# Causal attention with whole-array sums, queries and keys copied to SBUF, squares on GpSimd, and the output norm's roots behind the query's

## The chip, the cores and the metric

The kernel runs on one core of one Trainium2 chip. The metric is the device time of one execution in microseconds (us), the median of several runs. The core has a matrix engine, TensorE (PE in the rows; PEld is its loading of weights), VectorE (DVE), ScalarE (ACT), GpSimd (POOL) and SyncE (SP), which issues most DMAs. Every engine runs its own list of instructions in order, and semaphores order the engines among each other. Operands lie in SBUF; TensorE's products land in PSUM, which has eight banks of 512 fp32 columns.

## What is computed

Two decoder layers over 64 sequences of 128 tokens with 128 channels. The change touches one of their six parts, the second layer's causal self-attention with 16 query heads of 64 and one shared head of keys and values:

```python
xn = layernorm(x, g1)
q = xn @ Wq.T
kv = xn @ Wkv.T
k, v = (kv[..., :DIM_HEAD], kv[..., DIM_HEAD:])
q = q.reshape(b, n, HEADS, DIM_HEAD).transpose(0, 2, 1, 3)
q = q * SCALE
q, k = (l2norm(q), l2norm(k))
...
sim = jnp.einsum('bhid,bjd->bhij', q, k)
...
sim = jnp.where(causal_mask, max_neg, sim)
attn = jax.nn.softmax(sim.astype(jnp.float32), axis=-1).astype(sim.dtype)
out = jnp.einsum('bhij,bjd->bhid', attn, v)
...
out = out @ Wout.T
return layernorm(out, g2)
```

The caller adds the result to x and norms the sum again. Everything is fp32.

## The kernel before

The program runs its parts one after another, each over all tokens: a state-space scan, a preparation of weights, cross-attention, a gelu network, causal attention (`causal_phase`), a single-head attention and a last network. Names of tiles begin with the part's letter, `d_` in causal attention. A tile is channels (128 partitions) by tokens.

`causal_phase` takes 32 groups of two sequences (256 tokens, `N`). Each engine's list is written by hand as a function `step` of eight slots (`k` from 0 to 7); `drive` calls it for the first groups, then in a loop whose body is two groups, then for the last ones. In the steps of group `g`, the engine does work of `g` itself (`main`), the norm, keys and first queries of `g + 1` (`front`), and the output of `g - 1` (`tail`). Small tables say which piece stands in which slot.

- **Pieces.** A group has five: piece 0 are the keys, 1 to 4 the queries of four heads each (two products of 256 columns into one bank `pq`). `project` makes a piece in slot `QUERY`. In slot `LENGTH`, ScalarE squares it (`squares`, from PSUM into `sq`), TensorE sums the squares over a head's 64 channels (`lengths`, into `pn`), and VectorE takes the maximum with a small number (into `ln`). In slot `UNIT`, ScalarE makes the inverse root with `Ln` and `Exp` (`roots`), and VectorE multiplies `pq` by it: line 1553 for keys (`kn`), line 1556 for queries (`qn`).
- **Units.** A group has four: eight heads of one sequence. In an even slot TensorE makes the scores (two products, even and odd heads on the upper and lower 64 rows of the array, line 1371); ScalarE takes `Exp` of each half (line 1513); GpSimd multiplies each half by the causal mask `keep` (line 1355). Three slots later, in an odd slot, `weighted` makes the sums with the values `vv` and with ones: four products of 64 output columns each, the even and odd heads side by side in one bank, `pattn` for values and `pden` for ones (line 1385). ScalarE makes 1/`pden` with `Ln` and `Exp`, VectorE multiplies (line 1583).
- **Output.** In slots 1 and 2, eight products add up the output of the group before into `pm`; slots 3 and 4 norm it (ScalarE's square, TensorE's mean at line 1453, `Ln`, `Exp`, VectorE's product at line 1589) and add x (line 1593); slot 5 takes the mean out (TensorE, line 1457), slot 6 makes the second variance (line 1461) and its inverse root (`Ln`, `Exp`), and slot 7 the product that is stored.

Every engine takes the pieces of a slot in the order in which `step` names them, so a wait in one piece holds what stands behind it on that engine.

## Time and profile before

| | before |
|---|---|
| runs (us) | 3443.01, 3429.18, 3422.32; median 3429.18 |
| profiled execution (us) | 3427.96, of it 3426.2 from first to last instruction |
| TensorE busy | 3085.8 us (90% of the span), 12374 products |
| ScalarE busy | 2024.2 us (59%) |
| VectorE busy | 1765.3 us (52%) |
| GpSimd busy | 1152.1 us (34%) |
| causal attention | from about 1740 to 2644 us of the span |
| in it, each engine in 2000 to 2100 us | TensorE 97.97, ScalarE 74.55, VectorE 38.77, GpSimd 36.78 us; clock 1.00 |

Busy time of TensorE counts each product from its start to its modelled end, and ends overlap the next start; how far apart starts are says more. An fp32 product stands in the trace as two passes, so "x4" is two products. In the order of time, rows of one line that follow each other are merged: start, time from the first start to the last end, engine, line, tiles, shapes, count. The time in brackets is the idle time of the engine before the row, and what ended it. A list of instructions shows the line, the operation and the tiles, with the semaphores waited for in brackets; `REGISTER_ALU` and `ISA` are steps of the engine's sequencer, which compute the value that a wait compares with.

### The profile page before, as it was taken

To read this page: it belongs to the slowest core of one execution; us is meant where nothing else is said; L and a number is where in the kernel's file an instruction comes from. 1 tells how busy PE (TensorE), PEld (TensorE's weight loads), DVE (VectorE), ACT (ScalarE), POOL (GpSimd) and SP (SyncE) were. 2 spreads that over 40 slices of the span, in tenths; PEclk is the share of its full clock that TensorE was granted. 3 is DMA by queue.
4 is the path that set the end of the run, shared out by engine and by line. 5 is a ranking of instruction groups with operands and counts; after the bars stand their busy time and mean duration, and the time that the engine had idled before them with its cause. 6 is when DMAs were issued, how large, how long until landed. Compare 5 with 4: busy or idle time off the path is not lost. (4 is left out here: it accounts for less than half of the span.)

```text
span 3426.2 us, 44444 instructions
## 1 busy us (share of the span) xinstructions
PE 3085.8 (90%) x12374; PEld 1646.6 (48%) x12374; DVE 1765.3 (52%) x2607; ACT 2024.2 (59%) x4072; POOL 1152.1 (34%) x954
## 2 busy tenths in 40 slices
PE   5888888799999999966779999999998879999998
PEld 2333333477777777722234444444444634444443
DVE  5999999455555555589933433333333521111111
ACT  5777776366666666545557777777775523333333
POOL 4788788122222222256623333333332100000000
PEclk8999999799999999988889999999999979999999
DMA  3545544000000000011100000000000300000000
GB/s 97 170 144 167 155 156 149 30 16 21 21 18 21 17 22 17 14 42 52 43 22 14 14 14 14 18 14 14 14 14 31 137 34 19 18 18 28 18 19 12
DMA packets 104265, 159.18 MB, mean 46 GB/s; under 512 B 11904, under 2 KB 44560, under 8 KB 104208
## 3 DMA queue, kind: packets, MB, share of 16 engines
q1 hardware_dynamic: 97872, 144.89, 12.5%
q10 hardware_dynamic: 6336, 13.60, 1.3%
q8 instruction: 26, 0.43, 0.1%
q14 instruction: 31, 0.25, 0.0%
HBM read 85.77 MB, written 4.72 MB: 26 GB/s over the span
## 5 line engine op out<-in xcount | busy, mean ns | idle before, releaser
L1355 POOL TENSOR_TENSOR d_pr<-d_pr,d_keep 128x512 f32<-128x512 f32 x256 | 320.4, 1273 | 566.7 <-ACT d_pr L1513 566.7
L770 POOL TENSOR_TENSOR b_pn<-b_e,b_inv 128x616 f32<-128x616 f32 x128 | 161.4, 1261 | 603.2 <-DVE b_inv L951 603.2
L256 POOL TENSOR_TENSOR a_bx<-a_bcopy,a_drive_u 128x512 f32<-128x512 f32 x256 | 320.2, 1271 | 18.1 <-DVE a_state L523 11.5
L523 DVE TENSOR_TENSOR_SCAN a_state<-a_decay,a_bx 128x512 f32<-128x512 f32 x256 | 311.0, 1215 | 5.7 <-POOL a_bx L256 5.4
L276 PE MATMUL a_py<-a_prod,consts 128*128 128x512 f32 x512 | 285.0, 640 | 2.8 <-DVE a_t L503 1.4
L1922 PE MATMUL f_ph<-f_hb,wb 128*128 128x512 f32 x512 | 232.8, 598 | 6.4 <-ACT f_hb L1955 6.4
L1922 PE MATMUL f_ph<-f_ha,wb 128*128 128x512 f32 x512 | 229.0, 596 | 2.3 <-DVE f_ha L1984 2.3
L454 ACT ACTIVATE a_decay<-a_delta,neg_a 128x508 f32<-128x508 f32 x256 | 174.5, 682 | 73.2 <-DVE a_state L523 73.0
L926 DVE TENSOR_REDUCE b_peak<-b_pscore 128x8 f32<-128x616 f32 x128 | 102.3, 799 | 215.7 <-PE b_pscore L807 215.7
L876 ACT ACTIVATE b_yy<-b_py,y_bias 128x154 f32<-128x154 f32 x512 | 169.4, 382 | 67.8 <-PE b_py L816 67.5
L1577 DVE TENSOR_SCALAR d_ln<-d_pn 128x512 f32<-128x512 f32 (+1 forms) x160 | 101.8, 636 | 197.6 <-PE d_pn L1408 197.6
L816 PE MATMUL b_py<-b_cf,wb 128*128 128x154 f32 x1024 | 191.1, 309 | 10.0 <-DMA b_cf<-ctx 5.4
L1408 PE MATMUL d_pn<-d_sq,consts 128*128 128x512 f32 (+1 forms) x320 | 168.8, 610 | 19.4 <-ACT d_sq L1476 18.9
L529 DVE TENSOR_TENSOR a_prod<-a_state,a_pc 128x512 f32<-128x512 f32 x256 | 175.9, 687 | 12.9 <-DVE a_state L523 1.0
L1513 ACT ACTIVATE d_pr<-d_pscore 128x512 f32<-128x512 f32 x256 | 139.0, 596 | 71.0 <-PE d_pscore L1371 69.4
L816 PEld LDWEIGHTS b_py<-b_cf,wb 128*128 128x128 f32 x1024 | 154.9, 191 | 52.7 <-issue 21.4
L1556 DVE TENSOR_TENSOR d_qn<-d_pq,d_ln 128x512 f32<-128x512 f32 x128 | 88.6, 692 | 173.0 <-ACT d_ln L1484 173.0
L288 PE MATMUL a_pc<-a_bc,sel 96*128 96x512 bf16 x256 | 106.4, 415 | 77.3 <-DVE a_prod L529 75.9
L889 ACT ACTIVATE b_pt_sb<-b_ptr 77x512 f32<-77x512 f32 x256 | 137.9, 588 | 50.2 <-PE b_ptr L825 50.2
L1981 DVE SCALAR_TENSOR_TENSOR f_th<-f_th,f_pa 128x512 f32<-128x512 f32 x64 | 44.0, 688 | 239.5 <-ACT f_th L1947 239.5
L1922 PEld LDWEIGHTS f_ph<-f_hb,wb 128*128 128x128 f32 x512 | 96.7, 191 | 135.0 <-issue 116.3
L1922 PEld LDWEIGHTS f_ph<-f_ha,wb 128*128 128x128 f32 x512 | 97.8, 191 | 126.8 <-issue 123.1
(281 smaller groups left out, 6492.0 us busy)
## 6 DMA issues: line engine op xcount, KB each, us to landing
a_bcopy<-rows SPq DMA_DIRECT2D x256, 256.0 KB, 3.5
wb<-in_wb ACTq DMA_DIRECT2D x14, 480.0 KB, 4.2
a_xf<-in_x SPq DMA_DIRECT2D x16, 256.0 KB, 4.2
a_xt<-in_x ACTq DMA_DIRECT2D x16, 256.0 KB, 3.6
x<-a_xo SPq DMA_DIRECT2D x16, 256.0 KB, 2.3
b_xf<-x SPq DMA_DIRECT2D x32, 128.0 KB, 2.0
b_xt<-x SPq DMA_DIRECT2D x32, 128.0 KB, 2.0
x<-b_xo SPq DMA_DIRECT2D x32, 128.0 KB, 2.0
```

Of the source, the lines that this page charges most:

```text
L256: gp.tensor_tensor(bx[:, k % 4, :], bcopy[:, k % 4, :], drive_u[:, p, :], ALU.mult).then_inc(*bxt.step("bx"))
L276: mm(py[:], S["ident"][:], prod[:, j % 4, :], start=j == 0, stop=j == SLOTS - 1).then_inc(*pey.step("y"))
L454: A(b4(decay[k % 2][:])[:, :, 1:SEQ], b4(delta[:, p, :])[:, :, 1:SEQ], ACT.Exp, scale=S["neg_a"][:, k:k + 1]).then_inc(*exp_t.step("decay"))
L523: V.tensor_tensor_scan(state[:, j % 2, :], decay[j % 2][:], bx[:, j % 4, :], 0.0, ALU.mult, ALU.add).then_inc(*vs.step("scan"))
L529: V.tensor_tensor(prod[:, j % 4, :], state[:, j % 2, :], pc[j % 2][:], ALU.mult).then_inc(*vs.step("prod"))
L770: gp.tensor_tensor(heads(pn[:, j % 2, :]), heads(e[:, j % 2, :]), over(inv[:, j % 2, :], CTX), ALU.mult).then_inc(*pnt.step("n"))
L816: op = mm(py[:, NC * h:NC * (h + 1)], W["at"][:, 128 * (2 * i + h):128 * (2 * i + h + 1)], cf[:, q, :], start=True, stop=True)
L876: op = A(yy[:, q, :, 2 * i + h, :], py[:, NC * h:NC * (h + 1)].rearrange("p (b k) -> p b k", b=NB), ACT.Identity, bias=S["y_bias"][:, 2 * ...
L1355: gp.tensor_tensor(half, half, keep[:].unsqueeze(1).to_broadcast([128, QP, SEQ]), ALU.mult).then_inc(*gmt.step(f"m{odd}"))
L1408: mm(pn[:, 0:w], S["pair"], sq[:, bank, 0:w], start=True, stop=True).then_inc(*pen.step("n"))
L1513: A(pr[:, j % 2, odd, :], pscore[:, 512 * odd:512 * (odd + 1)], ACT.Exp, scale=16.0).then_inc(*ext.step(f"e{odd}"))
L1922: op = mm(ph[k % 2][:], w[:, i, 128 * c:128 * (c + 1)], src, start=i == 0, stop=i == FC - 1)
```

## The change

Four things change in `causal_phase`.

1. **Sums.** `vv` holds ones, values, ones side by side for each sequence. `weighted` makes two products of 128 output columns: for even heads with values and ones, for odd heads with ones and values. `pattn` has two banks, one for even and one for odd heads; in each, half of the partitions are sums with values and the other half sums with ones. ScalarE takes `Ln` in two instructions of 64 partitions, and VectorE multiplies in two.
2. **Copies.** VectorE copies each piece of queries from `pq` to `qc` and the keys to `kc`, both in SBUF. `kn` and `qn` are made from the copies. `project` waits for the copy that frees its bank instead of for the product.
3. **Squares.** The queries' squares are made by GpSimd from `qc`, in the odd slots behind the masks; the keys' by ScalarE from `kc`.
4. **Order.** `project` stands ahead of `weighted` in the odd slots. The second variance's `Ln` and `Exp` move from slot 6 on ScalarE to slot 7 behind `roots`, and VectorE's last product ahead of the unit's sums.

```diff
+        qc = sb("qc", [128, 2, 2 * N])
+        kc = sb("kc", [128, N])
         qn = sb("qn", [128, 2, PAIRS, N])
-        vv = sb("vv", [128, 2, NB, DH])
-        ones = sb("ones", [128, DH])
+        vv = sb("vv", [128, 2, NB, 3, DH])
         keep = sb("keep", [128, SEQ])
...
-        pattn = ps("pattn")
-        pden = ps("pden")
+        pattn = ps("pattn", 1024)
...
+        def query(gu, i):
+
+            return UNITS * gu + i - 1
...
+                        if k % 2:
+                            if u := piece(QUERY, g, p, k, front, main):
+                                gu, pu, i, r, bank = u
+                                pool.wait_ge(*vcp.at("q", query(gu, i)))
+                                if begun(r - 2):
+                                    pool.wait_ge(*pen.at("n", r - 2))
+                                gp.tensor_tensor(sq[:, bank, :], qc[:, i % 2, :], qc[:, i % 2, :], ALU.mult
+                                                 ).then_inc(*psq.step("sq"))
...
-                    for bank, w in ((pattn, vv[:, p, b, :]), (pden, ones[:])):
-                        for odd in range(2):
-                            op = mm(bank[64 * odd:64 * odd + 64, :], w, pr[:, j % 2, odd, :], start=True, stop=True,
-                                    skip_group_check=True)
-                    op.then_inc(*pea.step("a"))
+                    for odd in range(2):
+                        w = vv[:, p, b, 1 - odd:3 - odd, :].rearrange("p i d -> p (i d)")
+                        mm(pattn[:, 512 * odd:512 * (odd + 1)], w, pr[:, j % 2, odd, :], start=True, stop=True
+                           ).then_inc(*pea.step(f"a{odd}"))
 
                 def project(gu, pu, i, r, bank):
...
-                    if begun(r - 2):
-                        pe.wait_ge(*vpt.at("unit", r - 2))
+                    if i == 2:
+                        pe.wait_ge(*kcp.at("k", gu))
+                    elif begun(query(gu, i) - (1 if i < 2 else 2)):
+                        pe.wait_ge(*vcp.at("q", query(gu, i) - (1 if i < 2 else 2)))
...
                 def lengths(gu, pu, i, r, bank):
-                    pe.wait_ge(*sqt.at("sq", r))
                     if i == 0:
+                        pe.wait_ge(*ksq.at("sq", gu))
                         pe.wait_ge(*vf.at("v", gu))
                     else:
+                        pe.wait_ge(*psq.at("sq", query(gu, i)))
                         pe.wait_ge(*vmx.at("max", r - 1))
                     w = N if i == 0 else 2 * N
...
+                        if k % 2:
+                            if u := piece(QUERY, g, p, k, front, main):
+                                project(*u)
...
-                        if u := piece(QUERY, g, p, k, front, main):
-                            project(*u)
+                        if k == 2:
+                            if u := piece(QUERY, g, p, k, front, main):
+                                project(*u)
...
-                    w = N if i == 0 else 2 * N
-                    act.wait_ge(*pep.at("p", r))
+                    act.wait_ge(*kcp.at("k", gu))
                     if begun(r - 2):
                         act.wait_ge(*pen.at("n", r - 2))
-                    A(sq[:, bank, 0:w], pq[bank][:, 0:w], ACT.Square).then_inc(*sqt.step("sq"))
+                    A(sq[:, bank, 0:N], kc[:], ACT.Square).then_inc(*ksq.step("sq"))
...
-                        if u := piece(LENGTH, g, p, k, front, main):
-                            squares(*u)
+                        if k == 3:
+                            if u := piece(LENGTH, g, p, k, front, main):
+                                squares(*u)
+                        if tail and k == 7:
+                            act.wait_ge(*peo.at("var2", g - 1))
+                            A(t3[:], pm[:, N:2 * N], ACT.Ln, bias=S["eps"]).then_inc(*so.step("ln2"))
+                            act.wait_ge(*so.at("ln2", g - 1))
+                            A(t3[:], t3[:], ACT.Exp, scale=-0.5).then_inc(*so.step("rstd2"))
                         if front and k == 0:
...
-                        if u := summed(g, p, k, main, tail):
-                            _, _, j, r = u
-                            act.wait_ge(*pea.at("a", r))
+                        done = summed(g, p, k, main, tail)
+                        if done:
+                            _, _, j, r = done
                             if begun(r - 1):
                                 act.wait_ge(*vat.at("n", r - 1))
-                            A(den[:], pden[:], ACT.Ln).then_inc(*sdt.step("ln"))
+                            for odd in range(2):
+                                act.wait_ge(*pea.at(f"a{odd}", r))
+                                op = A(den[64 * odd:64 * odd + 64, :],
+                                       pattn[64 - 64 * odd:128 - 64 * odd, 512 * odd:512 * (odd + 1)], ACT.Ln)
+                            op.then_inc(*sdt.step("ln"))
+                        if done:
                             act.wait_ge(*sdt.at("ln", r))
                             A(den[:], den[:], ACT.Exp, scale=-1.0).then_inc(*sdt.step("inv"))
                         if k == 4:
...
-                        if tail and k == 6:
-                            act.wait_ge(*peo.at("var2", g - 1))
-                            A(t3[:], pm[:, N:2 * N], ACT.Ln, bias=S["eps"]).then_inc(*so.step("ln2"))
-                            act.wait_ge(*so.at("ln2", g - 1))
-                            A(t3[:], t3[:], ACT.Exp, scale=-0.5).then_inc(*so.step("rstd2"))
...
                     for k in range(SLOTS):
+                        if k % 2 and k != 3:
+                            if u := piece(QUERY, g, p, k, front, main):
+                                gu, pu, i, r, bank = u
+                                dve.wait_ge(*pep.at("p", r))
+                                if begun(query(gu, i) - 2):
+                                    dve.wait_ge(*psq.at("sq", query(gu, i) - 2))
+                                    dve.wait_ge(*vpt.at("unit", r - 2 if i > 2 else r - 3))
+                                V.tensor_copy(qc[:, i % 2, :], pq[bank][:]).then_inc(*vcp.step("q"))
                         if u := piece(UNIT, g, p, k, front, main):
                             gu, pu, i, r, bank = u
                             dve.wait_ge(*spt.at("rstd", r))
                             if i == 0:
-                                V.tensor_tensor(kn[:, pu, :], pq[bank][:, 0:N], ln[:, bank, 0:N],
+                                dve.wait_ge(*kcp.at("k", gu))
+                                V.tensor_tensor(kn[:, pu, :], kc[:], ln[:, bank, 0:N],
                                                 ALU.mult).then_inc(*vpt.step("unit"))
                             else:
+                                dve.wait_ge(*vcp.at("q", query(gu, i)))
                                 V.tensor_tensor(qn[:, pu, 2 * (i - 1):2 * i, :].rearrange("p i t -> p (i t)"),
-                                                pq[bank][:], ln[:, bank, :], ALU.mult).then_inc(*vpt.step("unit"))
+                                                qc[:, i % 2, :], ln[:, bank, :], ALU.mult).then_inc(*vpt.step("unit"))
+                        if k == 3:
+                            if u := piece(QUERY, g, p, k, front, main):
+                                gu, pu, i, r, bank = u
+                                dve.wait_ge(*pep.at("p", r))
+                                if begun(query(gu, i) - 2):
+                                    dve.wait_ge(*psq.at("sq", query(gu, i) - 2))
+                                    dve.wait_ge(*vpt.at("unit", r - 2 if i > 2 else r - 3))
+                                V.tensor_copy(qc[:, i % 2, :], pq[bank][:]).then_inc(*vcp.step("q"))
+                        if tail and k == 7:
+                            dve.wait_ge(*so.at("rstd2", g - 1))
+                            if begun(g - 2):
+                                dve.wait_ge(store, 16 * g - 16)
+                            V.tensor_tensor(xo[:, q, :], pm[:, 0:N], t3[:], ALU.mult).then_inc(*vo.step("out"))
                         if front and k == 2:
...
+                        if front and k == 2:
+                            r = PIECES * (g + 1)
+                            dve.wait_ge(*pep.at("p", r))
+                            if begun(g):
+                                dve.wait_ge(*ksq.at("sq", g))
+                                dve.wait_ge(*vpt.at("unit", r - PIECES))
+                            V.tensor_copy(kc[:], pq[(1 - p) % 2][:, 0:N]).then_inc(*kcp.step("k"))
                         if u := summed(g, p, k, main, tail):
                             gu, pu, j, r = u
                             hh, b = j // 2, j % 2
                             dve.wait_ge(*sdt.at("inv", r))
-                            V.tensor_tensor(attn[:, pu, QP * hh:QP * (hh + 1), SEQ * b:SEQ * (b + 1)],
-                                            pattn[:].rearrange("p (i t) -> p i t", i=QP),
-                                            den[:].rearrange("p (i t) -> p i t", i=QP), ALU.mult
-                                            ).then_inc(*vat.step("n"))
+                            for odd in range(2):
+                                half = slice(64 * odd, 64 * odd + 64)
+                                op = V.tensor_tensor(
+                                    attn[half, pu, QP * hh:QP * (hh + 1), SEQ * b:SEQ * (b + 1)],
+                                    pattn[half, 512 * odd:512 * (odd + 1)].rearrange("p (i t) -> p i t", i=QP),
+                                    den[half, :].rearrange("p (i t) -> p i t", i=QP), ALU.mult)
+                            op.then_inc(*vat.step("n"))
                         if tail and k == 4:
```

Three places in the lists of the loop's body. First TensorE, slots 4 to 6, from the variance of the output (L1453, after the change L1474) to the scores of slot 6. Before:

```order
L1453 MATMUL d_pm<-d_t,consts 128x256 [waits d_so]
L1385 MATMUL d_pattn<-d_pr,d_vv 64x512 [waits d_vat,d_gmt]
L1385 MATMUL d_pattn<-d_pr,d_vv 64x512
L1385 MATMUL d_pden<-d_pr,d_ones 64x512 x2
L1397 MATMUL d_pq<-d_xn,wb 128x256 [waits d_vpt]
L1397 MATMUL d_pq<-d_xn,wb 128x256
L1456 ISA
L1457 MATMUL d_pm<-d_t,consts 128x256 [waits d_vo]
L1367 ISA
L1371 MATMUL d_pscore<-d_qn,d_kn 128x512 [waits d_vpt,d_ext]
L1371 MATMUL d_pscore<-d_qn,d_kn 128x512
```

and with the change:

```order
L1473 ISA
L1474 MATMUL d_pm<-d_t,consts 128x256 [waits d_so]
L1413 MATMUL d_pq<-d_xn,wb 128x256 [waits d_kcp]
L1413 MATMUL d_pq<-d_xn,wb 128x256
L1400 MATMUL d_pattn<-d_pr,d_vv 128x512 [waits d_vat,d_gmt]
L1400 MATMUL d_pattn<-d_pr,d_vv 128x512
L1477 ISA
L1478 MATMUL d_pm<-d_t,consts 128x256 [waits d_vo]
L1382 ISA
L1386 MATMUL d_pscore<-d_qn,d_kn 128x512 [waits d_vpt,d_ext]
L1386 MATMUL d_pscore<-d_qn,d_kn 128x512
```

The projection (L1397, now L1413) moved ahead of the sums (L1385, now L1400), and of the four sums two are left, with the whole array.

Second VectorE, from the keys' product in slot 4 to the queries' product in slot 5. Before:

```order
L1553 TENSOR_TENSOR d_kn<-d_pq,d_ln 128x256 [waits d_spt]
L1576 REGISTER_ALU
L1577 TENSOR_SCALAR d_ln<-d_pn 128x512 [waits d_pen]
L1588 ISA
L1589 SCALAR_TENSOR_TENSOR d_t<-d_pm,wb,d_t 128x256 [waits d_so]
L1591 ISA
L1592 REGISTER_ALU [waits d_vo]
L1593 TENSOR_TENSOR d_t<-d_t,d_xt 128x256 [waits d_load_t]
L1551 ISA
L1556 TENSOR_TENSOR d_qn<-d_pq,d_ln 128x512 [waits d_spt]
```

and with the change:

```order
L1587 REGISTER_ALU [waits d_spt]
L1588 TENSOR_TENSOR d_kn<-d_kc,d_ln 128x256 [waits d_kcp]
L1626 TENSOR_SCALAR d_ln<-d_pn 128x512 [waits d_pen]
L1647 ISA
L1648 SCALAR_TENSOR_TENSOR d_t<-d_pm,wb,d_t 128x256 [waits d_so]
L1650 ISA
L1651 REGISTER_ALU [waits d_vo]
L1652 TENSOR_TENSOR d_t<-d_t,d_xt 128x256 [waits d_load_t]
L1578 REGISTER_ALU
L1582 COPY d_qc<-d_pq 128x512 [waits d_vpt,d_psq,d_pep]
```

`d_kn` reads the copy `d_kc` instead of `d_pq`, and in front of it stands a step of its own that waits for the roots (`d_spt`); behind the addition (L1593, now L1652) comes the copy of the next queries (L1582), and only then `d_qn`.

Third GpSimd, where before only pairs of masks (`d_pr`) followed each other, slots 0 to 1 of the loop's body with the change:

```order
L1362 TENSOR_TENSOR d_pr<-d_pr,d_keep 128x512 [waits d_ext]
L1360 REGISTER_ALU
L1362 TENSOR_TENSOR d_pr<-d_pr,d_keep 128x512 [waits d_ext]
L1367 REGISTER_ALU
L1369 ISA [waits d_vcp]
L1370 TENSOR_TENSOR d_sq<-d_qc 128x512 [waits d_pen]
```

Behind each pair of masks stands one square (`d_sq`), which waits for VectorE's copy (`d_vcp`) and for the lengths that last read its buffer (`d_pen`).

## Rows read from the trace of the kernel before

**Rows 1.** Windows of a middle stretch: busy time (instructions) by engine, granted clock, DMA.
```profile
core 0: us, PE busy (x) PEld busy (x) DVE busy (x) ACT busy (x) POOL busy (x), PEclk, DMA share, GB/s
...
2000.00:2100.00 100.00, 97.97 (x386) 48.08 (x385) 38.77 (x69) 74.55 (x145) 36.78 (x30) 1.00 0.05 16
```

**Rows 2.** Line L1553, window 1830 to 2590: count, min/median/max ns, first and last start.
```profile
L1553 DVE TENSOR_TENSOR d_kn<-d_pq,d_ln x28: 424/425/425, 1830.1 to 2569.3; 128x256 f32<-128x256 f32 x28
```

**Rows 3.** Order of time, TensorE, slots 4 to 8: start us, us, engine, line, tiles.
```profile
2155.45 1.13 PE L1371 MATMUL d_pscore<-d_qn,d_kn 64*128 64x512 f32 x4
...
2156.51 1.12 PE L1408 MATMUL d_pn<-d_sq,consts 128*128 128x512 f32 x2
...
2157.48 0.59 PE L1453 MATMUL d_pm<-d_t,consts 128*128 128x256 f32 x2
...
2158.00 1.08 PE L1385 MATMUL d_pattn<-d_pr,d_vv 128*64 128x512 f32 x4
...
2158.91 1.03 PE L1385 MATMUL d_pden<-d_pr,d_ones 128*64 128x512 f32 x4
...
2159.87 1.13 PE L1397 MATMUL d_pq<-d_xn,wb 128*128 128x256 f32 x4
...
2160.84 0.59 PE L1457 MATMUL d_pm<-d_t,consts 128*128 128x256 f32 x2
...
2161.36 1.13 PE L1371 MATMUL d_pscore<-d_qn,d_kn 64*128 64x512 f32 x4
...
2162.99 1.12 PE L1408 MATMUL d_pn<-d_sq,consts 128*128 128x512 f32 x2 [0.50 <-ACT d_sq L1476]
...
2166.34 1.13 PE L1397 MATMUL d_pq<-d_xn,wb 128*128 128x256 f32 x4
...
2167.65 1.13 PE L1371 MATMUL d_pscore<-d_qn,d_kn 64*128 64x512 f32 x4 [0.18 <-DVE d_qn L1556]
```

**Rows 4.** Order of time, TensorE, slot 2 of the next group, no switch inside.
```profile
2176.88 1.89 PE L1412 MATMUL d_pm<-d_attn,wb 128*128 128x256 f32 x8
...
2178.60 0.59 PE L1393 MATMUL d_pq<-d_xn,wb 128*128 128x256 f32 x2
```

**Rows 5.** Order of time, ScalarE and VectorE, slots 4 to 8 of the same group.
```profile
2156.63 1.09 ACT L1513 ACTIVATE d_pr<-d_pscore 128x512 f32<-128x512 f32 x2 [0.47 <-PE d_pscore L1371]
...
2158.59 0.42 DVE L1553 TENSOR_TENSOR d_kn<-d_pq,d_ln 128x256 f32<-128x256 f32 x1 [2.53 <-ACT d_ln L1484]
...
2158.93 0.68 DVE L1577 TENSOR_SCALAR d_ln<-d_pn 128x512 f32<-128x512 f32 x1
...
2159.53 0.47 DVE L1589 SCALAR_TENSOR_TENSOR d_t<-d_pm,wb,d_t 128x256 f32<-128x256 f32 x1
...
2160.14 0.43 DVE L1593 TENSOR_TENSOR d_t<-d_t,d_xt 128x256 f32<-128x256 f32 x1
...
2164.15 0.69 DVE L1577 TENSOR_SCALAR d_ln<-d_pn 128x512 f32<-128x512 f32 x1 [1.25 <-PE d_pn L1408]
...
2165.41 0.61 ACT L1482 ACTIVATE d_ln<-d_ln 128x512 f32<-128x512 f32 x1
...
2166.06 0.72 ACT L1484 ACTIVATE d_ln<-d_ln,d_shift 128x512 f32<-128x512 f32 x1
...
2166.82 0.69 DVE L1556 TENSOR_TENSOR d_qn<-d_pq,d_ln 128x512 f32<-128x512 f32 x1 [1.97 <-ACT d_ln L1484]
```

**Rows 6.** Line L1355, window 2155 to 2161: the two masks of slot 4.
```profile
L1355 POOL TENSOR_TENSOR d_pr<-d_pr,d_keep x2: 1272/1274/1276, 2157.3 to 2158.5; 128x512 f32<-128x512 f32 x2
```

**Rows 7.** Order of time near 2622: two masks merged, and VectorE's addition L1593.
```profile
2620.22 2.50 POOL L1355 TENSOR_TENSOR d_pr<-d_pr,d_keep 128x512 f32<-128x512 f32 x2 [3.29 <-ACT d_pr L1513]
...
2622.00 1.00 DVE L1593 TENSOR_TENSOR d_t<-d_t,d_xt 128x256 f32<-128x256 f32 x1
```

**Rows 8.** Line L770, cross-attention, whole trace: GpSimd's product.
```profile
L770 POOL TENSOR_TENSOR b_pn<-b_e,b_inv x128: 1216/1217/1414, 680.9 to 1446.4; 128x616 f32<-128x616 f32 x128
```

**Rows 9.** Line L614, weights' preparation: copies from PSUM, 512 columns.
```profile
L614 DVE COPY wb<-p_wo x2: 681/686/691, 645.9 to 646.6; 128x512 f32<-128x512 f32 x2
```

More of the change, by code:

```diff
@@ L1266, in causal_phase @@
         pen = tr("pen", "n")
-        sqt = tr("sqt", "sq")
+        ksq = tr("ksq", "sq")
+        kcp = tr("kcp", "k")
+        vcp = tr("vcp", "q")
+        psq = tr("psq", "sq")
         vmx = tr("vmx", "max")
@@ L1339, in _ @@
                 gp = nc.gpsimd
-                gp.memset(ones[:], 1.0).then_inc(*made.step("ones"))
+                gp.memset(vv[:], 1.0).then_inc(*made.step("ones"))
                 gp.memset(shift[:], 0.5 * SHIFT * float(np.log(2.0))).then_inc(*made.step("shift"))
```

19 lines of the change are left out of this document (7 added, 12 removed).

## The prediction

> **What bounds it.** I read the stages first. In the middle of causal attention TensorE is busy 97.97 of 100 us at the full clock, ScalarE 74.55, GpSimd 36.78, VectorE 38.77 [rows 1]. The stage does one group of two sequences after another; the keys' product L1553 starts 28 times from 1830.1 to 2569.3 us, so a group takes 739.2 / 27 = 27.38 us [rows 2], and 32 of them are about a quarter of the span. A busy TensorE is not one that streams, so next I read the order of time of one group from the scores of slot 4 (t = 0 at 2155.45) to those of the next slot 0 (t = 12.20) [rows 3], against a stretch in which nothing stops it [rows 4].
>
> In that stretch eight passes of 256 columns take 2178.60 - 2176.88 = 1.72 us, so 0.43 for two, 0.86 for four or for one 512-column product. In [rows 3] the same work takes longer wherever the array's shape changes: var to the sums 2158.00 - 2157.48 = 0.52 (0.09 more), values' sums 0.91 (0.05 more), ones' sums to projection 0.96 (0.10 more), the projection behind it 0.97 (0.11 more). That is 0.35 us a unit, 4 x 0.35 = **1.40 a group**. Two real waits are left: scores to lengths takes 1.06 in slot 4, so slot 6's lengths could have started at 2161.36 + 1.06 = 2162.42 and started at 2162.99 (0.57); the projection at 2166.34 and its 0.97 + 0.09 let the scores start at 2167.40, and they started at 2167.65 behind L1556 (0.25) [rows 3, 5]. Together 0.82. Without either a group would take 27.38 - 1.40 - 0.82 = 25.16 us: at most 2.22 x 32 = 71 us is to be had here.
>
> **What the change removes.** (a) *Whole-array sums.* Four products of 64 output columns, two at a time, become two of 128: four passes, 4 x 0.43 = 1.72 us, as much as before without the switches. The 1.40 goes: in all four units the sums stand between whole-array products now, and where slot 7's will stand before the scores, that switch is paid already, behind the projection. (b) *Squares to GpSimd, roots before the output's norm.* These aim at the 0.57 and the 0.25: four squares of 512 leave ScalarE, but four more `Ln` of 512 come (each half is its own instruction). The nearest row for both is `Ln` L1482 with 0.61 [rows 5], so ScalarE's load stays near 75 of 100. (c) *Copies and halves.* VectorE gets four copies of 512 (0.68 each, as L614 [rows 9]), one of 256 (0.42, as L1553), and a second half-product in each unit. A half has 64 partitions with 512 elements each: between 0.35 (half of L1556's 0.69) and 0.69 if the elements of a partition set it, as they do between 256 (0.42) and 512 (0.69) columns; I take 0.69. So 4 x 0.68 + 0.42 + 4 x 0.69 = 5.9 us a group come on 10.6 (38.77% of 27.38), 60% of a group. GpSimd's four squares (1.27 each, as a mask; by L770 between 1.22 and 1.41 [rows 6, 8]) bring it from 10.1 to 15.2, 55%. No engine's load passes TensorE's; what counts is where each piece stands.
>
> **Where the stall goes.** `kn` and `qn` were PSUM times SBUF; they become SBUF times SBUF. What that can cost the trace shows once for exactly these two engines: at 2622.00 the addition L1593, both of whose inputs lie in SBUF, was issued while the second of two GpSimd masks ran. It took 1.00 us, not the 0.43 that it takes at 2160.14, and ended at 2623.00, 0.28 behind the mask's end at 2620.22 + 2.50 = 2622.72 [rows 5, 7]. So such an operation is held to the end of the mask, and then needs 0.28 for 256 columns (about 0.55 for 512). The other way round, GpSimd's L770 takes 1.414 instead of 1.217 where it meets an operation of VectorE [rows 8].
>
> *`kn`, slot 4.* It is issued at t = 2158.59 - 2155.45 = 3.14; the second mask starts at 2158.5 and takes 1.27, to t = 4.3 [rows 5, 6]. With a second wait in front (L1593 starts 0.13 behind L1589's end, where one wait costs 0.03) it comes at 3.24, well into that mask. Both follow the same exponentials, so the change moves neither against the other. `kn` ends at 4.3 + 0.28 = 4.6, not at 3.56: **1.05 late**. Queued behind it on VectorE stand slot 4's maximum, the norm L1589, the addition L1593 and now slot 5's copy of queries. The addition ends at 2160.57 (5.12) + 1.05 = 6.17, TensorE takes it 0.14 later (as L1556's end 2167.51 to the scores), 6.31. The centring stands at 5.39 now and without the switches is due at 5.04: **wait 1.27**.
>
> *Lengths, slot 6.* Now due at 2162.42 - 2155.45 - 0.35 + 1.27 = 7.89. The copy follows the addition's start by 0.4: 6.1 to 6.8; the square could start at 6.95. But the product `qn` of slot 5 is ready first: maximum 4.5 to 5.2, roots 1.4 (0.65 + 0.72 and 0.03), 0.13 for two waits, so 6.77. It takes the port to 7.46, the square (1.27, as a mask) runs from about 7.3 to 8.6, lengths start at 8.65: **wait 0.77**, where 0.57 was.
>
> *Scores, slot 8.* Maximum 1.16 behind the lengths' start, 0.69, roots 1.43, two waits 0.10: the product at 8.65 + 3.38 = 12.03. The square next to it: lengths, var2 and projection 2.25, 0.2 until its result can be read (the 1.16 less 0.96 of passes), two more waits at the copy 0.2, copy 0.68, GpSimd 0.15: 12.13. By 0.1 us the product comes first and ends at 12.72; scores at 12.86, due at 12.20 - 0.82 - 0.70 (two units without switches) + 1.27 + 0.77 = 12.72: **wait 0.14**. The output norm's second roots, now in front of the query's on ScalarE, stand behind them and are out of this chain.
>
> *Slots 0 to 3* have cover. From slot 0's scores on, TensorE reaches the output's second half after 8.8 us (scores and lengths 2.0, var 0.43, projection 0.86, sums 1.72, half the output 1.72, scores and lengths 2.1). For it the last unit's sums have to be normed: they end at 5.0, ScalarE takes 0.61 + 0.65 for the second `Ln` and the `Exp`, VectorE 2 x 0.69, waits 0.4, so 7.7; ScalarE may come to them 0.3 late behind exponentials, roots and the input's norm. Cover 0.8 to 1.1; gone, each 0.1 a group costs 3 us. The squares of slots 1 and 3 follow a projection by 0.2 + 0.68 + 0.15 + 1.27 = 2.3 and, in slot 1, a mask that ends at 4.3; both end over 1 us before their lengths. Slot 1's product, if slot 1's square holds it to 6.2, still ends before the sums are to be normed.
>
> **Sum.** Out: 1.40 + 0.82 = 2.22. In: 1.27 + 0.77 + 0.14 = 2.18. That is -0.04 a group, -1 us for 32; the larger memset of `vv` at the start is under 1 us. From the profiled run's 3427.96 us (span 3426.2 and 1.8 around it) that gives 3427, and since the median of the runs is 1.2 above that one, **3428 us**: what the array's switches give back is spent on VectorE waiting for GpSimd.
>
> The Trainium skill, page "SBUF — State Buffer", section "Who interferes with whom", goes further than the row: a VectorE instruction with two SBUF inputs and a GpSimd instruction that reads SBUF exclude each other, whole instructions long, and the order of issue says who waits. The row agrees (0.43 becomes 1.00). By that rule the order at `kn` (mask first by 0.16) and at slot 7 (product first by 0.1) decides; it speaks against this change, and gives the same sum. No run here shows what happens between two GpSimd instructions that stand back to back.
>
> **Rivals.**
> - *Slower: the square of slot 7 gets in first.* The margin is 0.1 us, made of four small latencies. Then the product is held to 12.13 + 1.27 + 0.55 = 13.95, scores start at 14.1, 1.23 later: + 39 us, **3467**. It decides from the point where the copy comes 0.1 us sooner.
> - *Faster: `kn` isn't held*, because it finds the port free between the two masks (no row has two masks in front of such an operation with more behind). The addition ends at 5.22, centring waits 0.32, lengths 0.75 or, with the square ahead of the product, 0.44, scores 0.14: 1.21 or 0.9 for 2.22, 1.0 to 1.3 a group: -32 to -42 us, **3391**. For it: the masks overlap by 0.04. Against: the held addition.
> - *Faster still: nothing waits*; then 25.16 a group, -71, **3357**. Against: the first row of contention alone.
> - *The whole-array form doesn't give the switches back* (the second weights are not loaded ahead): + 45, **3472**. Against: the 0.86 for each whole-array product in [rows 4].
>
> **How the numbers follow.** Forecast 0.45 (its own range 3418 to 3440), slower rival 0.21, `kn` free 0.24, nothing waits 0.06, switches stay 0.04. The likeliest is 3428; 3383 to 3470 takes in the slower rival and `kn` free and leaves about 0.1 out. One per cent, about what a measurement can tell here, is 34 us, so 3394 and 3463: faster takes 0.19 of `kn` free (its middle is 3391) and all of nothing waits, 0.25; slower 0.21 + 0.04 = 0.25; within 1% the forecast and the rest of `kn` free, 0.50.
>
> **What would show it.** Groups of `kn` 27.3 us apart; `kn` at about 1.4 us instead of 0.42, ending 0.28 behind a mask; TensorE waiting for VectorE's addition at the centring, for GpSimd's square in slot 6, and no longer for ScalarE; the two sums 0.86 each, 1.72 from the first to whatever follows. A `kn` of 0.42 makes the forecast wrong to the fast side, a query product of 2 us in slot 7 to the slow side.

## The result, and the profile after

The changed kernel takes 3470.82 us (median of 3465.43 to 3474.07, four runs) against 3428.2 for the kernel before on the same chip: ratio 1.0124, 95% interval 1.0104 to 1.0143. It is slower, 0.8 us beyond the upper end of the range. The profiled execution took 3472.41 us, 3470.7 of it from first to last instruction.

The windows' row that answers to [rows 1], and the count that answers to [rows 2], of the kernel after:

```profile
2000.00:2100.00 100.00, 90.56 (x308) 48.05 (x307) 69.14 (x100) 74.01 (x141) 50.12 (x42) 1.00 0.03 12
```

```profile
L1588 DVE TENSOR_TENSOR d_kn<-d_kc,d_ln x27: 1396/1401/1406, 1835.6 to 2580.3; 128x256 f32<-128x256 f32 x27
```

TensorE falls from 97.97 to 90.56 us in 100, VectorE rises from 38.77 to 69.14. `kn` is held: 1.40 us each time, not 0.42. A group takes (2580.3 - 1835.6) / 26 = 28.64 us where it took 27.38: 1.26 more, x 32 = 40 of the 43 us that were lost.

TensorE's order of time, slots 4 to 8 of one group (slot 8 is slot 0 of the next) and on to the next slot 4 (start us, us, engine, line, tiles; in brackets idle time and its releaser), against [rows 3]:

```profile
2147.41 1.13 PE L1386 MATMUL d_pscore<-d_qn,d_kn 64*128 64x512 f32 x4
...
2150.73 1.88 PE L1400 MATMUL d_pattn<-d_pr,d_vv 128*128 128x512 f32 x4
...
2153.76 0.70 PE L1478 MATMUL d_pm<-d_t,consts 128*128 128x256 f32 x2 [1.15 <-DVE d_t L1652]
...
2154.39 1.13 PE L1386 MATMUL d_pscore<-d_qn,d_kn 64*128 64x512 f32 x4
...
2156.02 1.12 PE L1425 MATMUL d_pn<-d_sq,consts 128*128 128x512 f32 x2 [0.50 <-POOL d_sq L1370]
...
2158.27 1.88 PE L1400 MATMUL d_pattn<-d_pr,d_vv 128*128 128x512 f32 x4
...
2161.00 1.13 PE L1386 MATMUL d_pscore<-d_qn,d_kn 64*128 64x512 f32 x4 [0.85 <-DVE d_qn L1592]
...
2164.32 1.88 PE L1400 MATMUL d_pattn<-d_pr,d_vv 128*128 128x512 f32 x4
...
2170.24 1.89 PE L1429 MATMUL d_pm<-d_attn,wb 128*128 128x256 f32 x8
...
2176.05 1.13 PE L1386 MATMUL d_pscore<-d_qn,d_kn 64*128 64x512 f32 x4
```

The centring (L1478) is due when the sums are through, 2150.73 + 1.72 = 2152.45, and starts at 2153.76: 1.31 late, where 1.27 was forecast. Slot 6's lengths are due at 2154.39 + 1.06 and start at 2156.02: 0.57 (forecast 0.77). The scores of slot 8 are due at 2158.27 + 1.72 + 0.09 = 2160.08 and start at 2161.00: 0.92 (forecast 0.14). From the centring to slot 6's scores it is 2154.39 - 2153.76 = 0.63, where it was 0.52 before. Slots 0 to 3 take 2176.05 - 2161.00 = 15.05; the forecast left them 14.48 (its 25.16 for a group without switches and waits, less 12.20 - 0.82 - 0.70 = 10.68 for slots 4 to 7).

### The profile page after: what moved, and what is told of

Same layout as the page of the kernel before. It is cut to its first block and busy times, and to the rows that moved or that the text cites. A ratio compares the mean times of both kernels' runs of the same rounds, so it can differ in the third digit from the quotient of the medians.

```text
span 3470.7 us, 44461 instructions
## 1 busy us (share of the span) xinstructions
PE 3061.8 (88%) x11862; PEld 1677.5 (48%) x11862; DVE 2049.7 (59%) x2895; ACT 2037.1 (59%) x4072; POOL 1300.4 (37%) x1082
## 5 line engine op out<-in xcount | busy, mean ns | idle before, releaser
L770 POOL TENSOR_TENSOR b_pn<-b_e,b_inv 128x616 f32<-128x616 f32 x128 | 161.3, 1260 | 605.4 <-DVE b_inv L951 605.4
L1641 DVE TENSOR_TENSOR d_attn<-d_pattn,d_den 64x512 f32<-64x512 f32 x256 | 176.3, 689 | 134.0 <-ACT d_den L1553 132.2
L1400 PE MATMUL d_pattn<-d_pr,d_vv 128*128 128x512 f32 x512 | 242.5, 596 | 5.7 <-DVE d_attn L1641 5.7
L1370 POOL TENSOR_TENSOR d_sq<-d_qc 128x512 f32<-128x512 f32 x128 | 146.0, 1140 | 181.6 <-DVE d_qc L1582 94.3
L1502 ACT ACTIVATE d_ln<-d_ln 128x512 f32<-128x512 f32 (+1 forms) x160 | 94.1, 588 | 172.6 <-DVE d_ln L1626 172.6
L1548 ACT ACTIVATE d_den<-d_pattn 64x512 f32<-64x512 f32 x256 | 151.2, 591 | 36.3 <-PE d_pattn L1400 33.0
L1386 PE MATMUL d_pscore<-d_qn,d_kn 64*128 64x512 f32 x512 | 145.5, 645 | 28.5 <-DVE d_qn L1592 28.5
```

What stands on the lines that cost most here:

```text
L1400: mm(pattn[:, 512 * odd:512 * (odd + 1)], w, pr[:, j % 2, odd, :], start=True, stop=True).then_inc(*pea.step(f"a{odd}"))
L1641: op = V.tensor_tensor(attn[half, pu, QP * hh:QP * (hh + 1), SEQ * b:SEQ * (b + 1)], pattn[half, 512 * odd:512 * (odd + 1)].rearrange("p ( ...
```

## What ScalarE and VectorE do meanwhile

The order of time of these two engines in the same group, after, from `kn` to the output's first half on TensorE. Slot 4's exponentials, which start the keys' roots, stand first. Copies, slot 6's exponentials, operations that nothing below waits for, and the last `Exp` of three pairs (L1519, L1553, L1504) are left out:

```profile
2148.59 1.08 ACT L1539 ACTIVATE d_pr<-d_pscore 128x512 f32<-128x512 f32 x2 [0.25 <-PE d_pscore L1386]
...
2150.64 1.40 DVE L1588 TENSOR_TENSOR d_kn<-d_kc,d_ln 128x256 f32<-128x256 f32 x1 [0.88 <-ACT d_ln L1504]
...
2152.07 0.69 DVE L1626 TENSOR_SCALAR d_ln<-d_pn 128x512 f32<-128x512 f32 x1
...
2152.80 0.63 ACT L1502 ACTIVATE d_ln<-d_ln 128x512 f32<-128x512 f32 x1 [1.47 <-DVE d_ln L1626]
...
2153.46 0.72 ACT L1504 ACTIVATE d_ln<-d_ln,d_shift 128x512 f32<-128x512 f32 x1
...
2154.20 1.19 ACT L1548 ACTIVATE d_den<-d_pattn 64x512 f32<-64x512 f32 x2
...
2155.43 0.63 ACT L1553 ACTIVATE d_den<-d_den 128x512 f32<-128x512 f32 x1
...
2156.09 1.39 DVE L1641 TENSOR_TENSOR d_attn<-d_pattn,d_den 64x512 f32<-64x512 f32 x2 [1.10 <-ACT d_den L1553]
...
2157.51 0.69 DVE L1626 TENSOR_SCALAR d_ln<-d_pn 128x512 f32<-128x512 f32 x1
...
2158.24 0.63 ACT L1502 ACTIVATE d_ln<-d_ln 128x512 f32<-128x512 f32 x1 [0.93 <-DVE d_ln L1626]
...
2158.90 0.72 ACT L1504 ACTIVATE d_ln<-d_ln,d_shift 128x512 f32<-128x512 f32 x1
...
2159.53 0.45 ACT L1517 ACTIVATE d_t<-d_pm,eps_t 128x256 f32<-128x256 f32 x1
...
2160.45 1.19 ACT L1548 ACTIVATE d_den<-d_pattn 64x512 f32<-64x512 f32 x2
...
2162.34 1.39 DVE L1641 TENSOR_TENSOR d_attn<-d_pattn,d_den 64x512 f32<-64x512 f32 x2 [1.06 <-ACT d_den L1553]
...
2163.76 0.69 DVE L1626 TENSOR_SCALAR d_ln<-d_pn 128x512 f32<-128x512 f32 x1
...
2164.49 0.63 ACT L1502 ACTIVATE d_ln<-d_ln 128x512 f32<-128x512 f32 x1 [0.90 <-DVE d_ln L1626]
...
2165.78 0.45 ACT L1527 ACTIVATE d_u<-d_pm,eps_t 128x256 f32<-128x256 f32 x1
...
2166.29 1.99 PE L1429 MATMUL d_pm<-d_attn,wb 128*128 128x256 f32 x8
```

Read it as one chain: from `kn` on, every operation starts within 0.1 us of the end of the one that it follows. `kn` holds the maximum, the maximum the roots, the roots stand ahead of the two logarithms on ScalarE, these release the two half-products, which stand ahead of the next maximum on VectorE, and so on through two units, to the logarithm of the input's variance (L1527), for which the output's first half waits (due at 2164.32 + 1.72 = 2166.04, it starts 0.25 later). From there TensorE runs without a stop for 9.76 us to the next slot 4, whose exponentials release the next `kn`, 3.23 later (2150.64 - 2147.41). 15.65 + 9.76 + 3.23 = 28.64: **the chain closes into a loop, and its length is the group's time**. Any path from one `kn` to the next has that length; what makes this one the bound is that no link of it has slack. The products of slots 5 and 7, held or not, are not on it. That is the theory to test; the rivals are single causes: the order at the port in slot 7 (the port is short for what a VectorE operation with two SBUF inputs and a GpSimd operation don't get at the same time, as at `kn`), the sums' second logarithm and product, or VectorE's plain load. The expectations of the runs up to e11 still argue from the port and from single queues; e12's is the first that argues from the chain.

## The experiments

The group's time is read from the first and last `kn` between 1830 and 2600 us, as in [rows 2].

| run | us | ratio to before (95%) | group, us |
|---|---|---|---|
| before | 3428.2 | | 27.38 |
| after | 3470.8 | 1.0124 (1.0104 to 1.0143) | 28.64 |
| e1 `kn` behind the addition | 3423.1 | 0.9992 (0.9981 to 1.0002) | 27.24 |
| e2 queries' products from PSUM | 3468.0 | 1.0122 (1.0105 to 1.0139) | 28.64 |
| e3 both | 3417.3 | 0.9969 (0.9955 to 0.9983) | 27.06 |
| e4 before, with the sums alone | 3460.1 | 1.0111 (1.0084 to 1.0137) | 28.54 |
| e5 e3, input's norm out of the queue | 3397.7 | 0.9927 (0.9906 to 0.9947) | 26.23 |
| e6 e4 and the order of the roots | 3459.0 | 1.0098 (1.0081 to 1.0114) | 28.29 |
| e7 after, with the old sums | 3470.2 | 1.0137 (1.0112 to 1.0162) | 28.72 |
| e8 e2, one half-product of two | 3421.9 | 0.9990 (0.9979 to 1.0001) | 27.16 |
| e9 after, slot 7's product first | 3466.5 | 1.0108 (1.0084 to 1.0131) | 28.65 |
| e10 e5, the row on VectorE split | 3379.9 | 0.9853 (0.9831 to 0.9874) | 25.84 |
| e11 e5, with the old sums | 3409.9 | 0.9943 (0.9921 to 0.9965) | 26.74 |
| e12 after, slot 4 nearly unmasked | 3438.4 | 1.0036 (1.0022 to 1.0050) | 27.67 |

**e1, `kn` behind the addition**

```diff
 # VectorE, step, slot 4
-kn = kc * ln            # ahead of maximum, norm, addition
 maximum; norm; addition
+kn = kc * ln
```

> The changed kernel with one product moved on VectorE: the keys' product `kn` of slot 4 stands behind that slot's maximum, norm and addition instead of ahead of them, where GpSimd's two masks of the slot are over. Same work, same engine, another place. Theory (the port): `kn` takes 0.43 us instead of 1.40, the addition of the residual ends about 1.4 us earlier, and the centring's wait of 1.3 us falls to 0.1 to 0.3; about 1.0 us a group, 3432 to 3442 us, by the runs' 3471 of the changed kernel. Rival (VectorE has simply 6 us more work in a group and is late by its sum): moving a product within the slot changes little, 3462 to 3475 us, and `kn` takes what it took.

3423.1 us, faster than the range, and 1.40 us a group less than after. `kn` takes 0.42 there. TensorE's waits for others in e1 (summed us between 1830 and 2600, times, longest):

```profile
PE d_pscore L1386 <- DVE d_qn L1590: 22.8, 28, 0.9
PE d_pn L1425 <- POOL d_sq L1370: 21.0, 28, 0.9
```

The wait at the centring is gone; the two others stay, 0.8 a group each. The load theory falls: the same work in another place costs 48 us less.

**e2, queries' products from PSUM**

```diff
-qn = qc[i % 2] * ln
+qn = (pq[bank] if i < 4 else qc[i % 2]) * ln
 # project, pieces 0, 3 and 4
+wait for the product two pieces back
```

> The changed kernel, but the queries' products of the first three pieces of each group read the queries where the projection left them, in PSUM, as the kernel before did; the copy to SBUF stays and feeds GpSimd's square alone. A projection waits for the product two pieces back where it overwrites its bank. Theory (the port): these products take 0.69 us everywhere, in slot 7 the one that was held for 1.20 behind the square no longer is, scores of the next slot 0 wait 0.1 to 0.3 instead of 0.92, the wait in slot 6 falls by some 0.3: 3440 to 3452 us. Rival (what delays the scores in slot 7 is only that the second half-product keeps VectorE from the maximum): the wait at slot 0's scores falls by the held part alone, 0.5 us or less, and slot 6 doesn't move: 3454 to 3466 us.

A miss: 3468.0 us, and the group takes 28.64 as in after. Slots 6 to 8 in e2, order of time of VectorE and TensorE:

```profile
2006.15 1.12 PE L1427 MATMUL d_pn<-d_sq,consts 128*128 128x512 f32 x2
...
2006.60 1.39 DVE L1644 TENSOR_TENSOR d_attn<-d_pattn,d_den 64x512 f32<-64x512 f32 x2 [1.10 <-ACT d_den L1555]
...
2008.03 0.69 DVE L1629 TENSOR_SCALAR d_ln<-d_pn 128x512 f32<-128x512 f32 x1
...
2010.25 0.69 DVE L1594 TENSOR_TENSOR d_qn<-d_pq,d_ln 128x512 f32<-128x512 f32 x1 [0.94 <-ACT d_ln L1506]
...
2011.00 1.13 PE L1386 MATMUL d_pscore<-d_qn,d_kn 64*128 64x512 f32 x4 [0.72 <-DVE d_qn L1594]
```

The product isn't held any more (0.69), and the scores still wait 0.72: the maximum starts 1.88 behind the lengths, right behind the two half-products. What the port no longer takes here, the chain takes.

**e3, both edits** (the diffs of e1 and e2 together)

> The two edits together: `kn` behind the addition, and the queries' products of three pieces from PSUM. Theory (the port makes both waits): the gains add, 1.0 and 0.7 to 1.0 us a group: 3395 to 3415 us, faster than either kernel. Rival (one wait hides the other, so that the removed one comes back downstream at slot 7's scores or at the output): 3420 to 3440 us.

3417.3 us, just above the range: faster than either kernel, by 0.3% against before. With `kn` out of the chain the other edit is worth 0.18 a group.

**e4, the sums alone, and e6, the sums with the new order of the roots** (both from the kernel before; e6 leaves `project` in its old place)

```diff
 # e4: weights [values, ones] or [ones, values], 128 columns, two products
-for bank, w in ((pattn, vv), (pden, ones)): for odd in 0, 1: mm(bank[64 * odd:64 * odd + 64], w, pr[odd])
+for odd in 0, 1: mm(pattn[:, 512 * odd:512 * odd + 512], vv[1 - odd:3 - odd], pr[odd])
 # Ln and the product with 1/den: once for each half
 # e6, besides:
+roots of the output's norm behind the query's in slot 7, its product ahead of slot 7's half-products
```

> The kernel before with the first part of the change alone: weights of values and ones together, two whole-array products of 128 output columns, two halves of the logarithm and two half-products; no copies, no squares on GpSimd, the old order. Theory: the four switches of the array's shape are saved (1.40 us a group), against them stand a second logarithm on ScalarE (0.61) and a second half-product on VectorE (0.69) in each unit, which delay lengths in slot 6 and scores in slot 8 by at most 0.6 each where ScalarE was already late: 3383 to 3412 us. Rival (ScalarE, 75% busy and late twice in a group, can't take four more logarithms: its waits grow by what TensorE saves): 3420 to 3440 us. Rival (the switches aren't saved): 3450 us or more.

> The whole-array sums alone (e4) with the order part of the change as well: the roots of the output's norm behind the query's roots of slot 7, its product ahead of the half-products; no copies, squares on ScalarE. In e4 TensorE waited 1.35 and 0.42 us a group for ScalarE's squares, 0.5 for slot 7's product, 0.27 for the output's product. Theory: the roots of slot 7 start 0.5 earlier, so the scores' 0.5 and the output's 0.27 go, the squares' waits stay: 0.7 to 0.8 us a group, 3430 to 3440 us. Rival (what the scores win, the squares lose, since ScalarE is 82% busy): 3450 to 3462 us.

e4 misses by 48 us to the slow side: the sums alone lose 34 us against the kernel before on the same chip (3426.1). Its time lies in the last rival's range, but the switches are saved, as TensorE's order shows (1.72 us from the sums to the projection); it is ScalarE's rival at a higher price, as its waits and the windows' row show:

```profile
2003.92 1.88 PE L1383 MATMUL d_pattn<-d_pr,d_vv 128*128 128x512 f32 x4
2005.64 1.03 PE L1394 MATMUL d_pq<-d_xn,wb 128*128 128x256 f32 x4
```

```profile
PE d_pn L1405 <- ACT d_sq L1473: 48.9, 54, 1.4
PE d_pscore L1369 <- DVE d_qn L1556: 12.9, 27, 0.5
PE d_pm L1426 <- DVE d_xo L1601: 7.3, 27, 0.3
```

```profile
2000.00:2100.00 100.00, 89.76 (x303) 48.42 (x303) 47.29 (x79) 82.26 (x157) 34.93 (x28) 1.00 0.05 16
```

TensorE stands 1.8 us a group behind ScalarE's squares, which stand behind four more logarithms. In e6 the waits for the product and for L1426 go and that for the squares grows to 70.5 us (2.6 a group): the rival was right. So neither the squares on ScalarE nor the sums' extra work had the room that a load of 75 in 100 suggests.

**e7, the changed kernel with the old sums**

```diff
 # sums, logarithm and product as in the kernel before; copies, GpSimd's squares and the order as after
```

> The changed kernel with the old sums: four products of 64 columns in pairs, one logarithm and one half of the products on the sums; copies, squares on GpSimd and the order stay. Theory (the port costs by itself what the change lost): `kn` still 1.4 us, the centring waits about 1 us, slot 7's product is held or just free; with 1.40 us of switches back the group takes 28.4 to 29.1 us: 3460 to 3490 us, as slow as the changed kernel or slower. Rival (the sums' second logarithm and half-product made the loss, as the run with the sums alone was 34 us slower than before): 3425 to 3445 us.

3470.2 us, in the theory's range. Slots 6 to 8 in e7, order of time of three engines:

```profile
2007.27 1.12 PE L1428 MATMUL d_pn<-d_sq,consts 128*128 128x512 f32 x2 [0.50 <-POOL d_sq L1372]
...
2008.43 0.69 DVE L1626 TENSOR_SCALAR d_ln<-d_pn 128x512 f32<-128x512 f32 x1 [1.13 <-PE d_pn L1428]
...
2010.58 1.04 POOL L1372 TENSOR_TENSOR d_sq<-d_qc 128x512 f32<-128x512 f32 x1 [0.59 <-DVE d_qc L1582]
...
2010.66 1.50 DVE L1592 TENSOR_TENSOR d_qn<-d_qc,d_ln 128x512 f32<-128x512 f32 x1 [0.24 <-ACT d_ln L1507]
```

Here the maximum follows the lengths by 1.16 and the product by 3.39, as forecast (1.16 and 3.38), and the square still wins, by 0.08: it comes at 3.31, not 3.48. Copies, squares and order lose as much by themselves as the whole change, and beside them the new sums win nothing.

**e8, one half-product of two left out**

```diff
-for odd in range(2):
+for odd in range(1):    # attn zeroed once at the start
     attn[half] = pattn[half, 512 * odd:512 * odd + 512] * den[half]
```

> The run with the queries' products from PSUM (e2) once more, with the second half-product of each unit left out, so that the upper 64 partitions of the normed sums stay zero (they are zeroed once at the start). There the product of slot 7 was no longer held, yet the scores behind it still waited 0.72 us: the maximum came right behind the two half-products. Theory (the half-products stand ahead of the maximum in VectorE's queue and keep it): with one of them gone the maximum comes 0.7 earlier and the wait at slot 0's scores falls to 0.1 or less, while the wait of 1.15 at the centring stays: 0.6 to 0.9 us a group, 3440 to 3450 us. Rival (the roots on ScalarE or the lengths set the product there): the wait stays above 0.5, 3458 to 3470 us.

3421.9 us: 46 less than e2, twice what was expected, since both pairs on the chain get shorter, not only the one in front of slot 6's maximum. The one wait that is left on TensorE is that behind `kn`:

```profile
PE d_pm L1481 <- DVE d_t L1656: 29.9, 29, 1.0
```

**e9, slot 7's product ahead of the square**

```diff
 # GpSimd, slot 7, before the square
+wait for VectorE's product of slot 7
```

> The changed kernel with one wait more: GpSimd's square of slot 7 waits until VectorE's product of slot 7 is done, so the product always comes first, as the prediction had it. Theory: the product isn't held (0.69 instead of 1.20), but it starts no sooner, since the maximum stands behind the second half-product: scores of the next slot 0 wait 0.49 instead of 0.92, the lengths behind them about 0.1 for the later square: 0.3 to 0.43 us a group, 3455 to 3462 us, and not the 3428 that was forecast for this order. Rival (the order at the port was the whole miss): the wait falls to 0.14, 3440 to 3448 us. Rival (the square's delay costs as much at the lengths): 3466 to 3473 us.

3466.5 us, a miss by 4 us. The time lies in the last rival's range. TensorE in e9:

```profile
2014.00 1.13 PE L1388 MATMUL d_pscore<-d_qn,d_kn 64*128 64x512 f32 x4 [0.34 <-DVE d_qn L1594]
2015.19 1.13 PE L1427 MATMUL d_pn<-d_sq,consts 128*128 128x512 f32 x2
...
2019.80 1.99 PE L1431 MATMUL d_pm<-d_attn,wb 128*128 128x256 f32 x8 [0.27 <-ACT d_u L1529]
```

The scores come 0.5 sooner relative to their due time. The lengths lose little of it to the later square (0.13: 2014.00 + 1.06 = 2015.06, start 2015.19), so that rival's reason isn't the one; but the output's first half (L1431) waits for the same logarithm on ScalarE as before, and the group takes 28.65. The order in slot 7, at which the forecast saw its decision, decides nothing.

**e12, slot 4 nearly unmasked**

```diff
-mask all 128 columns
+w = 4 if k == 4 else SEQ; mask columns 0 to w
```

> The changed kernel with `kn` where the change put it, but with GpSimd's two masks of slot 4 cut to 4 columns of 128 in each sequence, so that one unit of four is left nearly unmasked (its sums are not causal). Everything else is as in the changed kernel, the masks of slots 0, 2 and 6 too. Theory (`kn` is held by these two masks, and it stands in an unbroken chain of VectorE and ScalarE that sets the group): `kn` takes 0.42 to 0.6 us instead of 1.40, the centring's wait falls from 1.3 to 0.3 or 0.4, about 1.0 us a group, 3436 to 3446 us. Rival (what the run with `kn` behind the addition won came from the product's place ahead of the maximum, not from the masks): `kn` stays long or the time does, 3462 to 3474 us.

3438.4 us, 0.97 a group less, as forecast by the chain. `kn` in its old place, in e12:

```profile
L1590 DVE TENSOR_TENSOR d_kn<-d_kc,d_ln x27: 425/426/426, 1855.0 to 2574.5; 128x256 f32<-128x256 f32 x27
```

So the masks hold it. The 0.43 by which e1 is better still is `kn`'s own duration, which e1 takes off the chain.

**e5, the input's norm out of ScalarE's queue, and e10, the row on VectorE split**

```diff
 # e5 = e3, and
+GpSimd squares the input (slot 0); ScalarE: roots of its variance ahead of the query's roots in slot 1
 # e10 = e5, and on VectorE
-slot 5: half-product 0, half-product 1;  slot 6: maximum
+slot 5: half-product 0;  slot 6: maximum, half-product 1   # each half has its own semaphore
+copy of slot 5 ahead of kn
```

> The run with both edits (e3: `kn` behind the addition, products from PSUM) with the input's norm taken out of ScalarE's queue in slots 0 and 1: its square on GpSimd, which is idle there, and its roots ahead of the query's roots of slot 1. In e3 the variance came 0.24 us late and the output's first half 0.43 behind ScalarE's logarithm of it, which stood behind roots. Theory: both waits go, 0.5 to 0.7 us a group, 3395 to 3402 us. Rival (ScalarE's queue only hands the delay on, to the half-products and the output's second half): 3410 to 3420 us.

> The fastest run so far (e5) with two moves on VectorE: slot 5's second half-product stands behind slot 6's maximum (the sums of slot 7 wait for each half by itself), and slot 5's copy ahead of `kn`. In e5 the lengths of slot 6 still wait 0.45 for the square, and the scores behind slot 7 0.19 for the product, since the two half-products and the maximum stand in a row. Theory: with the row shortened by 0.7 and the copy 0.35 sooner both waits go, 0.5 to 0.6 us a group: 3378 to 3386 us. Rival (the sums of slot 7 now wait for the second half, or `kn` is held by the earlier square and its slot pays): 3392 to 3402 us.

Both times lie in the theory's range: 3397.7 and 3379.9 us. e10 beats the kernel before by 1.5%. Its windows' row:

```profile
2000.00:2100.00 100.00, 99.12 (x343) 53.78 (x341) 68.39 (x110) 80.18 (x152) 58.99 (x52) 1.00 0.05 16
```

VectorE is as busy as in after (68.39 against 69.14), ScalarE and GpSimd busier, TensorE busy 99.12.

**e11, e5 with the old sums** (the diff of e7 on e5)

> The fastest run so far (e5) with the old sums: four products of 64 columns in pairs, one logarithm, one product on the sums. It says what the whole-array form is worth once the held products are gone. In e5 stretches without a wait show about 1.0 us a group less than the kernel before for the four sums (14.72 against 15.22 us for slots 0 to 3, 10.87 against 11.38 for slots 4 to 7), and 0.64 of waits that hang on the second half-product. Theory: 1.0 more for TensorE, 0.4 to 0.6 less of waits: 0.4 to 0.6 us a group, 3410 to 3418 us. Rival (as in the unrepaired kernel, where the old sums made no difference): 3393 to 3402 us. Rival (the whole 1.0 to 1.4): 3428 to 3442 us.

3409.9 us, at the edge of the range: with the chain out of the way the whole-array sums are worth 0.51 a group in the profiled executions. The times differ by 12 us, but were taken on two chips, and the intervals of the two ratios overlap.

## Why the prediction was wrong, step by step

In the terms of its sum, for one group: the 25.16 without switches and waits, and what stands on it.

| term | forecast | measured |
|---|---|---|
| centring behind `kn` | 1.27 | 1.31 |
| lengths, slot 6 | 0.77 | 0.57 |
| scores, slot 8 | 0.14 | 0.92 |
| slots 0 to 3 over 14.48 | 0 | 0.57 |
| centring to slot 6's scores, over 0.52 | 0 | 0.11 |
| sum | 2.18 | 3.48 |

The difference, 1.30, x 32 is 42 us, and 3428 + 42 is 3470.

- **`kn` held by the second mask: right**, to 0.05 us in duration, end and the wait at the centring. e1 and e12 confirm cause and price of the hold. By the Trainium skill, page "SBUF — State Buffer", section "Who interferes with whom", a VectorE instruction with two SBUF inputs and GpSimd's reads exclude each other; the 1.40 and 0.42 us agree.
- **"Maximum 1.16 behind the lengths' start": wrong.** It is 2157.51 - 2156.02 = 1.49 in after. The step took VectorE as free; unit 1's two half-products, which the sum had priced as load (4 x 0.69), stood in front. With one product instead of the two halves (e7) 1.16 is exact.
- **"By 0.1 us the product comes first": wrong**, and so the slower rival's order came about, near its 3467 us. In after, slot 7:

```profile
2159.34 1.05 POOL L1370 TENSOR_TENSOR d_sq<-d_qc 128x512 f32<-128x512 f32 x1
...
2159.74 1.20 DVE L1592 TENSOR_TENSOR d_qn<-d_qc,d_ln 128x512 f32<-128x512 f32 x1 [0.58 <-ACT d_ln L1504]
```

The square comes 3.32 behind the lengths, not 3.48, and the product 3.72 behind them, not 3.38; held, it ends 0.55 behind the square, as estimated for 512 columns. But the order is not why the kernel is slow: with the forecast order restored (e9) it still takes 3466.5. The rival named the right time by luck, for a reason that costs nothing here.
- **"Slots 0 to 3 have cover" of 0.8 to 1.1: wrong.** The sum is off (5.0 + 0.61 + 0.65 + 1.38 + 0.4 is 8.0, not 7.7), and it looked at the output's second half alone. There the last unit's sums are normed 8.99 us behind slot 0's scores, later than either figure, but the second half follows only at 9.24 (2170.24) and doesn't wait. The first half does: the second half-product of the unit before ends at 2162.34 + 1.39, 2.73 behind slot 0's scores, and the maximum and the roots behind it make L1527 late, for which the first half waits 0.25. e5, which takes this norm out of the queue, wins 20 us against e3.
- **1.40 from the switches: too much.** Where nothing waits, slots 0 to 3 take 14.72 us in e5 against 15.22 before, 0.50 for the 0.70 forecast. Over the group that is 1.0, and e11 finds 0.51 of it in the group's time. The rival in which none of it comes back named 3472, near the time too, but by e5's stretches most of it did come back.
- **The step behind these**: "No engine's load passes TensorE's; what counts is where each piece stands." The sum then followed TensorE's waits one by one, each with its neighbours on time. VectorE's 5.9 us of new work were costed for three places and called covered elsewhere. Nobody followed ScalarE and VectorE in turn until the chain closed.

How the loop fits the runs, worked out behind them from the rows of after (e12 alone was expected by it, at about 1.0 a group):

| run | what leaves the loop | expected a group | measured |
|---|---|---|---|
| e2, e9 | nothing (products aren't on it) | 0 | 0.00, +0.01 |
| e12 | the hold of `kn`, 1.40 - 0.43 | -0.97 | -0.97 |
| e1 | all of `kn`, 1.40 and 0.03 | -1.43 | -1.40 |
| e8 | two half-products of 0.70 | -1.40 | -1.48 |

e3, e5 and e10 go on from e1, whose edit takes `kn` off the loop; their gains were not worked out from it. e7 has a shorter loop (one logarithm and one product less in each unit) and isn't set by it: there the waits for the port (0.89, 0.66 and 0.50 a group) and the 1.0 of switches make the same time by another way. That the two agree within 0.1 us a group is, as far as these runs show, a coincidence. Why the centring stands 0.11 longer before the scores wasn't tried.

## What to carry to other kernels

When a change puts work on an engine that isn't the bound, don't stop at its load: follow the in-order queues of the two side engines in turn, piece by piece, until the chain comes back to where it began, and compare that loop with the bound engine's own time; while the loop is the longer of the two, what lies on it costs its full duration, and what lies beside it, held or not, costs nothing. An idle time of the bound engine doesn't say what its repair is worth. Two stood out here, 1.15 us a group at the centring and 0.85 at slot 8's scores: moving the one product behind the first (e1) was worth 48 us, and undoing the hold behind the second (e2, e9) nothing that stands clear of the noise. An operation that gains a second SBUF input should stand where GpSimd is idle: `kn` takes 0.42 us there (e1) and 1.40 behind the mask.

## What the runs showed of the hardware

- A VectorE operation that is held comes in between two of GpSimd's that stand back to back. After, order of time:

```profile
2170.02 1.59 DVE L1611 SCALAR_TENSOR_TENSOR d_xn<-d_xf,wb,d_u 128x256 f32<-128x256 f32 x1
2170.06 2.67 POOL L1362 TENSOR_TENSOR d_pr<-d_pr,d_keep 128x512 f32<-128x512 f32 x2 [3.38 <-ACT d_pr L1539]
```

It starts 0.04 ahead of the first mask, yet ends 0.28 behind that mask's 1.27, before the second one is through, and the pair takes 2.67 instead of 2.50. In e5 the same operation starts 0.13 ahead of the masks (2005.75 against 2005.88) and takes 0.48. Between the 0.04 and the 0.13 of these two runs the order turns. So the earlier start, by which the prediction decides who waits, didn't decide at 0.04.
- GpSimd's square of 512 columns, one tile read twice, takes 1.04 us where the mask takes 1.27; behind a VectorE product it takes 1.42 (2154.47, after).
